# Norms of the attention stage on POOL, statistics spread over steps, and first units in the node units' order

## The chip, the cores and the metric

The kernel runs on one core of a Trainium2 chip. The metric is the device time of one execution in microseconds (us). The engines are PE (TensorE: matmuls, transposes), DVE (VectorE), ACT (ScalarE), POOL (GpSimd) and SP (SyncE, which here only issues DMAs). They run their own instruction streams in order and meet at semaphores.

## The reference

Input x is (8, 512, 128) in fp32. Four layers follow each other, each `x = layernorm(x + layer(x))`:

```
x = ln(x + mamba_like(x))          # conv, gating, a scan over the batch axis
x = ln(x + mixture_of_8_experts(x))
x = ln(x + attention(x))           # 16 heads of 8, softmax over 512 tokens, no output projection
x = ln(x + dag_of_6_nodes(x))      # below
```

The last layer makes six nodes. Each takes three earlier nodes, passes them through an edge matrix and a bias, does an attention of 8 heads of 16, multiplies with Wo and adds the scaled result to q:

```
q = ew[c,0]*(nodes[in_q] @ We[eq] + be[eq]);  k, v likewise
nodes[c] = act_w[c] * (softmax(qh kh^T / 4) vh @ Wo[c]) + q
```

Node 5 is then normalised, multiplied by ln_g, ln_b is added, then the layer's input, and the sum is normalised again: that is the output.

## The kernel before, in words

The first two layers take up some 380 us. The change touches what comes after, the attention stage, which is a row of 64 units. A unit is one batch element and eight heads. Units 0 to 15 are *first units* (third layer: 8 batch elements times two halves of the heads), units 16 to 63 are *node units* (six nodes times 8). The last eight, 56 to 63, are *final units*: their output is normed. `at_(c, q, r)` gives unit 4q + r; `x.half` is 1 for the odd first units, which complete a batch element; `x.b` is the batch element; `final(x)` gives 0 to 7 for a final unit and None for another.

Each engine runs a `body(c, q, r)` for every unit, with an order written out by hand: two halves k (four heads each) of eight steps i. A step is written (k, i) below. In each step PE does two score matmuls (`scores`, L1035, into the two banks of bank_s), whose rows DVE reduces to a negated maximum (`reduce`, L1394), and two matmuls of transposed scores (`scoresT`, L1058, into one of the two slots of bank_x), from which ACT makes the exponentials (`exp`, L825). The score matmuls and reductions run 36 tiles ahead of the transposed ones (`LEAD`). A score matmul waits until the reduction two tiles back is done. `slot()` hands out the two slots of bank_x in turn; whoever takes one waits for the reader of the last content. `misc()` does the same for bank_m.

Further work hangs on certain steps:

- `output` (L1075), probabilities times values, into bank_o. In node units it is two calls per four heads and two key tiles with 512 columns each (steps 0, 1 and 4, 5), in first units four calls with 256 columns (steps 0 to 7). The third argument of `paced(x, node, first)` is the step in a first unit, the second the step in a node unit.
- `turn` (L1089) transposes the result after ACT's copy `ev_pv` (L793); DVE's `divide` (L1505, L1512) writes it, divided by the sums, to ctx_sb.
- `value`, `proj_q`, `proj_kh`, `proj_qh` (L1021, L987, L1000, L1008) project for later units; each takes a slot of bank_x, and ACT copies it out (L775, L746, L756 or L759, L767).
- Node units: `turn_ctx` (L1099) at (0,6) transposes ctx_sb into a slot of bank_x, ACT copies it (`ev_cT`, L801), `out_proj` (L1109) at (0,7) multiplies with Wo into bank_m, and DVE's `node_out` (L1525) at (1,0) adds q. `maxima` (L1045) at step 1 transposes the maxima into bank_m, ahead of the step's outputs; SP writes them from there (`rows_m`) for the transposed scores of the next half.
- Odd first units, done during the even unit that follows: DVE adds the residual (`residual` step 0, L1535) at (0,7), takes the statistics (L1274 four times, L1278 four times) at (1,0) and normalises (L1283 four times) at (1,3). In between POOL makes 1/std (`rstd`, L600 and L602). `turn_x3` (L1118) transposes the result at (1,7).
- Final units: DVE's `final_norm` takes statistics at (1,3) and normalises at (1,5) of the next unit, and does both again at (0,1) and (0,7) of the unit after; in between POOL does `rstd`, adds ln_b to x3 (L665), multiplies with ln_g (L667) and sums (L669) in `final_sum`. `turn_final` (L1129) at (1,1) is PE's part.
- POOL's `split` (L609, L611) makes two parts of k and q of the unit three ahead; SP stacks them (`stack`).

POOL's order in a unit is: rstd of the residual, final_sum, split, rstd of the last norm. SP's is: loads, store_out, rows_m, stack, store_x3.

The functions that the change touches:

Of the kernel before, what the change touches and what calls it, by code (L numbers as in the profile page):

```python
# [11 lines left out]
P = 128  # L12
# [39 lines left out]
def build(nc, a):  # L52
# [7 lines left out]
    with ExitStack() as ctx:  # L60
# [74 lines left out]
        ctx_sb = cut2(L)  # L135
        ctxT = cut2(L)
# [81 lines left out]
        def names(prefix, *ns):  # L218
            for n in ns:
# [16 lines left out]
              "x2in", "x3", "x3out", "mv", "rs", "ones")  # L236
# [75 lines left out]

        def paced(x, node, first):

            return node if x.c.node else first
# [44 lines left out]
        def _(sp):  # L360
# [190 lines left out]
            def body(c, q, r):  # L551
# [6 lines left out]
                store_out(at_(c, q, r - 2))  # L558
# [6 lines left out]
                store_x3(at_(c, q, r - 1))  # L565
            units(sp, body)
# [11 lines left out]
        def _(pool):  # L578
# [50 lines left out]
            def residual_rstd(x):  # L629
# [28 lines left out]
            def final_sum(x):  # L658
# [12 lines left out]
            def final_rstd(x):  # L671

                j = final(x)
                if j is None:
                    return
                rstd(mv2, rs20, rs2, eps_ln[:, :], (S["f_mv2"], j + 1), (S["f_rs2_link"], j + 1), S["f_rs2"])

            def body(c, q, r):
# [5 lines left out]
            end = at_(kn, QU - 1, RING - 1)  # L684
            final_sum(end)
            final_rstd(end)
# [5 lines left out]
        def _(act):  # L692
# [102 lines left out]
            def ev_cT(x):  # L795
# [5 lines left out]
                act.activation(ctxT, ring.take()[0][:, 0:L], ACT.Copy).then_inc(S["c_cT_ev"], 1)  # L801
# [103 lines left out]
        def _(pe):  # L905
# [156 lines left out]
            def output(x, k, kp, step, steps):  # L1062


                if x is None or not 0 <= step < steps:
                    return
                G = 2 * x.u + k
                j, cols = 2 * step // steps, slice(0, L) if steps == 2 else slice(step % 2 * L // 2, (step % 2 + 1) * L // 2)
                if step == 0:
# [4 lines left out]
                for h in range(GH):  # L1074
                    mm = pe.matmul(bank_o[COL * h:COL * (h + 1), cols], vaug[x.half][:, 2 * kp + j, GH * k + h, :],  # L1075
                                   PT[:, kp, h, j, cols], start=(kp == 0 and step == 0),
                                   stop=(kp == 1 and step == steps - 1))
                if step == steps - 1:
# [13 lines left out]
            def turn_ctx(x):  # L1092
# [4 lines left out]
                to = slot(S["c_cT_ev"], x.un + 1)  # L1097
                for t in range(NT):
                    mm = pe.transpose(to[:, t * P:(t + 1) * P], ctx_sb[:, t * P:(t + 1) * P], ident[:, :])  # L1099
# [118 lines left out]
            def body(c, q, r):  # L1218
                x, last, ahead = at_(c, q, r), at_(c, q, r - 1), at_(c, q, r + 3)
                steps = paced(x, 2, 4)  # L1220
                for k in range(2):
                    for i in range(8):
# [3 lines left out]
                        scores(*two)  # L1226
                        if i == 1:
                            maxima(*led_group(c, q, r, k))
                        output(*((last, 1) if k == 0 else (x, 0)), 1, i, steps)
                        output(x, k, 0, i - 4, steps)  # L1230
                        if i == paced(x, 3, 5):
                            turn(*((last, 1) if k == 0 else (x, 0)))
                        if k == 0:
                            if i == paced(x, 2, 7):
# [18 lines left out]
            for step in range(2):  # L1253
                output(end, 1, 1, step, 2)
# [9 lines left out]
        def _(dve):  # L1264
# [232 lines left out]
            def divide(x, k, step):  # L1497
# [12 lines left out]
                dst = ctx_sb.rearrange("p (t m) -> p t m", t=NT)[:, :, first:first + w]  # L1510
# [16 lines left out]
            def residual(x, step):  # L1527

                x = only(x, False)
                if x is None or not x.half:  # L1530
                    return
                if step == 0:
                    need(dve, S["c_x2in"], 16 * x.b + 16)
                    need(dve, S["c_ot_ev"], 4 * x.b + 4)
                    dve.tensor_tensor(ctx_sb, ctx_sb, x2s, ALU.add).then_inc(S["c_xlink"], 1)  # L1535
                if step == 1:
                    need(dve, S["c_xlink"], (NT + 1) * x.b + 1)
                    stats(ctx_sb, stt, mv, S["c_xlink"], (NT + 1) * x.b + 1, S["c_mv"])
                if step == 2:
                    need(dve, S["c_rs"], x.b + 1)  # L1540
                    need(dve, S["c_x3T_ps"], x.b)
                    need(dve, S["c_x3out"], 16 * x.b)
                    normalise(x3s, ctx_sb, mv, rs, S["c_x3"])

            def final_norm(x, step):

                j = final(x)
                if j is None:
                    return
                if step == 0:  # L1550
                    need(dve, S["f_tT_ev"], j + 1)
                    stats(nT, stt, mv, S["f_link"], NT * j, S["f_mv"])
                if step == 1:
                    need(dve, S["f_rs"], j + 1)
                    need(dve, S["f_y"], j)
# [106 lines left out]
```

## Time and profile before

| | |
|---|---|
| median of 3 runs | 2267.18 us (2262.42 to 2274.65) |
| profiled execution | 2264.24 us, span 2262.2 us |
| PE busy | 2081.8 us, 92% of the span |
| DVE busy | 1745.5 us, 77% |
| ACT busy | 1478.8 us, 65% |
| POOL busy | 341.8 us, 15% |
| mean granted clock of PE | 0.944 |

The span is the time from the first instruction to the last on the profiled core. Busy time is the union of an engine's instructions; matmuls are pipelined and their ends are modelled, so a busy PE isn't PE at its peak. A line such as L1283 is the line of the kernel that issued the instruction, which for norms is that of a helper. The granted clock is a share of 2.4 GHz; in the records it is either 1.0 or 0.5.

### The profile page before, as it was taken

Reading aid. Unit: us, or ns where it says so; the run is one execution under the profiler, and the core shown is the slowest. Engines: PE = TensorE matmul, PEld = TensorE weight load, DVE = VectorE, ACT = ScalarE, POOL = GpSimd, SP = SyncE. Lnnn points to the kernel's source line nnn. Section 1 sums busy time; section 2 is a strip of 40 time slices with the busy share of each in tenths; the row PEclk is TensorE's granted clock in tenths of the full one; section 3 lists DMA queues with packets and bytes.
Section 4 is the critical chain, followed back from the end, with each engine's and each line's share of the span. In section 5 each row is a group of like instructions: output and inputs, shape, how many; then the busy total and the mean of one; then the engine's idle time right before and its main releaser. Section 6 shows DMA issues by size and latency. Waiting matters only on the chain.

```text
span 2262.2 us, 34032 instructions
## 1 busy us (share of the span) xinstructions
PE 2081.8 (92%) x11820; PEld 868.5 (38%) x11820; DVE 1745.5 (77%) x3501; ACT 1478.8 (65%) x2004; POOL 341.8 (15%) x385
## 2 busy tenths in 40 slices
PE   6747886999999999999999999999999999999995
PEld 2224442444344443333443334333333343333332
DVE  5846887677778777777777777777777777778884
ACT  4733552566666667777777777777777777776664
POOL 1102222000000011111111111111111111113223
PEclk9977786799899999999999999999999999999998
DMA  3001114133233345565655556555665565655630
GB/s 101 19 23 60 49 50 72 44 72 71 53 66 70 77 96 109 115 107 107 107 108 105 109 107 107 107 108 107 108 107 107 105 109 106 109 107 98 97 57 24
DMA packets 137206, 195.76 MB, mean 87 GB/s; under 512 B 20153, under 2 KB 55633, under 8 KB 137041
## 3 DMA queue, kind: packets, MB, share of 16 engines
q1 hardware_dynamic: 137040, 193.63, 43.9%
q8 instruction: 95, 1.56, 0.3%
q14 instruction: 71, 0.57, 0.1%
HBM read 75.45 MB, written 23.73 MB: 44 GB/s over the span
## 4 chain that ended last, share of the span: by engine, by line
PE 74%; DVE 16%; issue 5%; ACT 3%; POOL 1%; DMA 0%; DVEq 0%; POOLq 0%; SPq 0%; ACTq 0%
PE bank_s L1035 24%; PE bank_o L1075 20%; DVE nm L1394 6%; PE bank_x L1058 6%; PE bank_m L1089 3%; PE bank_x L1021 3%; PE bank_x L1000 3%; PE bank_x L1008 2%; ACT big L825 2%; PE bank_x L987 2%; DVE big L1283 2%; PE bank_m L1109 2%; PE bank_x L1135 2%; DVE big L1525 1%; PE bank_s L938 1%
## 5 line engine op out<-in xcount | busy, mean ns | idle before, releaser
L1394 DVE TENSOR_REDUCE nm<-bank_s 128x1 f32<-128x512 f32 x2048 | 1337.0, 684 | 361.7 <-PE bank_s L1035 355.6
L825 ACT ACTIVATE big<-bank_x 128x1024 f32<-128x1024 f32 x1024 | 1047.1, 1023 | 462.8 <-PE bank_x L1058 447.4
L1035 PE MATMUL bank_s<-kst,qst 48*128 48x512 f32 x2048 | 848.7, 473 | 39.9 <-DVE nm L1394 36.2
L1058 PE MATMUL bank_x<-qst,kst 50*128 50x512 f32 x2048 | 755.6, 450 | 5.3 <-ACT big L825 1.9
L1035 PEld LDWEIGHTS bank_s<-kst,qst 48*128 48x128 f32 x2048 | 356.5, 188 | 711.6 <-DVE nm L1394 640.0
L1075 PE MATMUL bank_o<-big,at 128*32 128x512 f32 (+1 forms) x5104 | 582.4, 529 | 3.2 <-ACT big L825 2.0
L1058 PEld LDWEIGHTS bank_x<-qst,kst 50*128 50x128 f32 x2048 | 306.2, 188 | 29.0 <-ACT big L825 22.5
L609 POOL CAST at<-at 128x512 fp32r<-128x512 f32 x112 | 68.2, 609 | 1295.2 <-ACT at L756 1028.9
L1075 PEld LDWEIGHTS bank_o<-big,at 128*32 128x32 f32 x5104 | 102.3, 109 | 175.3 <-issue 155.7
L611 POOL TENSOR_TENSOR at<-at 128x512 fp32r<-128x512 f32 x112 | 143.3, 1279 | 10.0
L793 ACT ACTIVATE at<-bank_o 128x512 f32<-128x512 f32 x128 | 76.4, 597 | 37.5 <-PE bank_o L1075 37.5
L1089 PE MATMUL bank_m<-ident,at 128*128 128x128 f32 x512 | 85.8, 291 | 1.0 <-ACT at L793 0.7
L833 ACT ACTIVATE big<-bank_x,big 128x128 f32<-128x128 f32 x256 | 68.9, 377 | 27.2 <-issue 11.6
L600 POOL TENSOR_TENSOR big<-big,eps_ln 128x4 f32<-128x4 f32 x40 | 13.7, 341 | 459.2 <-DVE big L1278 459.2
L1283 DVE TENSOR_SCALAR big<-big 128x128 f32<-128x128 f32 x192 | 68.1, 469 | 15.7 <-POOL big L602 14.8
L1135 PE MATMUL bank_x<-xw,big 128*128 128x512 f32 x128 | 79.5, 768 | 0.0
L1089 PEld LDWEIGHTS bank_m<-ident,at 128*128 128x128 f32 x512 | 54.8, 143 | 50.2 <-issue 47.9
L1478 DVE TENSOR_REDUCE big<-big 128x128 f32<-128x1024 f32 x32 | 61.1, 1908 | 10.2 <-ACT big L833 9.9
L1008 PE MATMUL bank_x<-at 128*128 128x512 f32 x96 | 52.8, 632 | 3.5
L1109 PE MATMUL bank_m<-big,at 128*128 128x512 f32 x96 | 55.0, 655 | 0.7 <-issue 0.7
L1021 PE MATMUL bank_x<-at 128*128 128x128 f32 x384 | 55.6, 288 | 0.0
L987 PE MATMUL bank_x<-at 128*128 128x512 f32 x96 | 53.9, 643 | 0.8 <-ACT big L817 0.8
(151 smaller groups left out, 1501.8 us busy)
## 6 DMA issues: line engine op xcount, KB each, us to landing
at<-nodes_d SPq DMA_DIRECT2D x144, 256.0 KB, 5.2
kst<-at SPq DMA_DIRECT2D x288, 128.0 KB
qst<-at SPq DMA_DIRECT2D x288, 128.0 KB
nodes_d<-big SPq DMA_DIRECT2D x48, 256.0 KB, 3.0
at<-w_d SPq DMA_DIRECT2D x48, 193.0 KB, 5.2
at<-x2T_d SPq DMA_DIRECT2D x32, 256.0 KB, 4.3
kst<-at SPq DMA_DIRECT2D x128, 64.0 KB
qst<-at SPq DMA_DIRECT2D x128, 64.0 KB
```

The lines of the kernel that those rows point to most:

```text
L611: pool.tensor_tensor(dst[:, 1, :], src, dst[:, 0, :], ALU.subtract).then_inc(done, n)
L825: act.activation(PT[:, kp, h, :, :], ring.take()[0].rearrange("p (c n) -> p c n", c=2), ACT.Exp, scale=x.c.scale).then_inc(S["c_ex"], 1)
L987: pe.matmul(to[:, 0:L], t[:, 0:P], t[:, WA:WA + L], start=True, stop=True).then_inc(S["c_qT_ps"], 1)
L1021: mm = pe.matmul(to[:, k * n:(k + 1) * n], t[:, P + k * P:P + (k + 1) * P], w, start=True, stop=True)
L1035: pe.matmul(bank_s[:, n % 2, :], qst[rows, x.r, h, t * P:(t + 1) * P], kst[rows, x.r, h, :], start=True, stop=True).then_inc(S["c_s_ps"], 1)
L1058: mm = pe.matmul(sec(to, j), kst[rows, x.r, h, kc_ * P:(kc_ + 1) * P], qst[rows, x.r, h, :], start=True, stop=True)
L1075: mm = pe.matmul(bank_o[COL * h:COL * (h + 1), cols], vaug[x.half][:, 2 * kp + j, GH * k + h, :], PT[:, kp, h, j, cols], start=(kp == 0 an ...
L1089: mm = pe.transpose(bank_m[:, t * P:(t + 1) * P], ot_sb[:, t * P:(t + 1) * P], ident[:, :])
L1109: pe.matmul(bank_m[:, :], st_o[x.half][:, 0:P], ctxT, start=True, stop=True).then_inc(S["c_wo_ps"], 1)
L1135: mm = pe.matmul(sec(bank_x[:, t % 2, :], j), hT[:, t * P:(t + 1) * P], xw[:, j * 512:(j + 1) * 512], start=True, stop=True)
L1283: i = dve.tensor_scalar(dst[:, t * D:(t + 1) * D], src[:, t * D:(t + 1) * D], mv_[:, t, 0:1], rs_[:, t:t + 1], ALU.subtract, ALU.mult)
L1394: dve.tensor_reduce(nm[:, k, at_n:at_n + 1], bank_s[:, n % 2, :], AX.X, ALU.max, negate=True).then_inc(S["c_red"], 1)
```

## The change

- DVE's residual sum goes to POOL (`residual_sum`). For it ctx_sb gets a second buffer (`ctx_two`), by the batch element's parity.
- All normalisations of the attention stage go to POOL (`normalise` there, four tensor_scalar of 128x128 each).
- DVE's statistics are no longer one piece of eight instructions but six pieces of one bn_stats or two bn_aggr (`tile_stats`), put in the steps listed below.
- `paced` and the split of `output` into four calls go: first units have the order of node units. In all units `output` now stands before `maxima`.
- `turn_ctx` writes bank_m in place of a slot of bank_x.
- POOL's order is now residual_sum, residual_norm, final_out of the unit two back, split, final_sum; in final_sum the sum with ln_b comes first. SP's store_out stands at the end of the unit.

```diff
+        ctx_two = (ctx_sb, sb("ctx_odd", [P, L])[:, :])
 # SP
-                store_out(at_(c, q, r - 2))
                 ahead, nxt = at_(c, q, r + 3), at_(c, q, r + 1)
...
                 store_x3(at_(c, q, r - 1))
+                store_out(at_(c, q, r - 2))
 # POOL
+            def normalise(dst, src, mv_, rs_, done):
+                for t in range(NT):
+                    i = pool.tensor_scalar(dst[:, t * D:(t + 1) * D], src[:, t * D:(t + 1) * D], mv_[:, t, 0:1], rs_[:, t:t + 1],
+                                           ALU.subtract, ALU.mult)
+                i.then_inc(done, 1)
+            def residual_sum(x):
...
+                to = ctx_two[x.b % 2]
+                need(pool, S["c_x2in"], 16 * x.b + 16)
+                need(pool, S["c_ot_ev"], 4 * x.b + 4)
+                pool.tensor_tensor(to, to, x2s, ALU.add).then_inc(S["c_xsum"], 1)
+            def residual_norm(x):
...
                 rstd(mv, rs0, rs, eps_ln[:, :], (S["c_mv"], x.b + 1), (S["c_plink"], x.b + 1), S["c_rs"])
+                need(pool, S["c_rs"], x.b + 1)
+                need(pool, S["c_x3T_ps"], x.b)
+                need(pool, S["c_x3out"], 16 * x.b)
+                normalise(x3s, ctx_two[x.b % 2], mv, rs, S["c_x3"])
...
-                rstd(mv, rs0, rs, eps_node[:, :], (S["f_mv"], j + 1), (S["f_rs_link"], j + 1), S["f_rs"])
                 need(pool, S["f_x3_in"], 16 * (j + 1))
                 pool.tensor_tensor(x33, x33, b3, ALU.add).then_inc(S["f_plink"], 1)
+                rstd(mv, rs0, rs, eps_node[:, :], (S["f_mv"], j + 1), (S["f_rs_link"], j + 1), S["f_rs"])
+                need(pool, S["f_rs"], j + 1)
+                normalise(zn, nT, mv, rs, S["f_nm"])
...
             def body(c, q, r):
-                residual_rstd(at_(c, q, r - 1))
+                residual_sum(at_(c, q, r - 1))
+                residual_norm(at_(c, q, r - 1))
+                final_out(at_(c, q, r - 2))
+                split(at_(c, q, r + 3))
                 final_sum(at_(c, q, r - 1))
-                split(at_(c, q, r + 3))
-                final_rstd(at_(c, q, r - 1))
 # ACT
-                act.activation(ctxT, ring.take()[0][:, 0:L], ACT.Copy).then_inc(S["c_cT_ev"], 1)
+                act.activation(ctxT, bank_m[:, :], ACT.Copy).then_inc(S["c_cT_ev"], 1)
...
-                        if i == paced(x, 1, 3):
+                        if i == 1:
                             ev_pv(*((last, 1) if k == 0 else (x, 0)))
 # PE
-                to = slot(S["c_cT_ev"], x.un + 1)
+                misc(S["c_cT_ev"], x.un + 1)
...
+                        output(*((last, 1) if k == 0 else (x, 0)), 1, i)
+                        output(x, k, 0, i - 4)
                         if i == 1:
                             maxima(*led_group(c, q, r, k))
-                        output(*((last, 1) if k == 0 else (x, 0)), 1, i, steps)
-                        output(x, k, 0, i - 4, steps)
-                        if i == paced(x, 3, 5):
+                        if i == 3:
                             turn(*((last, 1) if k == 0 else (x, 0)))
                         if k == 0:
-                            if i == paced(x, 2, 7):
+                            if i == 2:
                                 value(at_(c, q, r + 1))
 # DVE
+            def tile_stats(src, st_, mv_, ready, link, base, done, step):
+                if step < NT:
+                    need(dve, *ready)
+                    dve.bn_stats(st_[:, step, :], src[:, step * D:(step + 1) * D]).then_inc(link, 1)
+                    return
+                need(dve, link, base + NT)
+                for t in (2 * (step - NT), 2 * (step - NT) + 1):
+                    i = dve.bn_aggr(mv_[:, t, :], st_[:, t, :])
+                if step == NT + 1:
+                    i.then_inc(done, 1)
...
-                            if i == paced(x, 4, 6):
+                            if i == 4:
                                 divide(*((last, 1) if k == 0 else (x, 0)), j)
...
+                        for step, place in enumerate(((0, 6), (0, 7), (1, 0), (1, 1), (1, 2), (1, 3))):
+                            if (k, i) == place:
+                                residual_stats(last, step)
+                        for step, place in enumerate(((1, 3), (1, 4), (1, 5), (1, 6), (1, 6), (1, 7))):
+                            if (k, i) == place:
+                                node_stats(last, step)
+                        for step, place in enumerate(((0, 4), (0, 5), (0, 6), (0, 7), (0, 7), (1, 0))):
+                            if (k, i) == place:
+                                sum_stats(older, step)
```

## Rows read from the trace of the kernel before

**Rows 1.** The chain that ended last, by engine (page, part 4).
```profile
PE 74%; DVE 16%; issue 5%; ACT 3%; POOL 1%; DMA 0%; DVEq 0%; POOLq 0%; SPq 0%; ACTq 0%
```
**Rows 2.** Windows: length, busy PE, PEld, DVE, ACT, POOL, clock, DMA, GB/s; units 7, 8, 30, 58.
```profile
610.40:637.30 26.90, 26.55 (x216) 11.33 (x220) 21.66 (x41) 18.61 (x23) 1.89 (x2) 1.00 0.33 85
637.30:668.60 31.30, 29.11 (x220) 12.49 (x224) 25.23 (x54) 19.22 (x24) 3.09 (x4) 0.95 0.31 58
1239.60:1267.70 28.10, 27.71 (x162) 11.14 (x165) 22.27 (x42) 20.73 (x25) 3.70 (x5) 1.00 0.50 108
2057.40:2089.00 31.60, 30.03 (x163) 11.78 (x162) 27.68 (x66) 21.30 (x27) 9.90 (x12) 1.00 0.58 104
```
**Rows 3.** Single lines: durations min/median/max in ns, first and last start; L1525 from 930.4 to 2026.7.
```profile
L1535 DVE TENSOR_TENSOR big<-big x8: 678/680/681, 469.7 to 882.5; 128x512 f32<-128x512 f32 x8
...
L1525 DVE SCALAR_TENSOR_TENSOR big<-bank_m,at x39: 739/742/743, 945.2 to 2013.4; 128x512 f32<-128x512 f32 x39
```
**Rows 4.** Timeline (start, length, idle before and its releaser): unit 8, then unit 62.
```profile
657.06 1.29 DVE L1394 TENSOR_REDUCE nm<-bank_s 128x1 f32<-128x512 f32 x2 [1.36 <-PE bank_s L1035]
658.27 2.01 DVE L1283 TENSOR_SCALAR big<-big 128x128 f32<-128x128 f32 x4
...
660.94 0.49 PE L1035 MATMUL bank_s<-kst,qst 48*128 48x512 f32 x1 [1.38 <-DVE nm L1394]
...
2206.26 0.86 DVE L1274 BATCH_NORM_STATS2 big<-big 128x6 f32<-128x128 f32 x4
...
2207.28 0.38 DVE L1278 BATCH_NORM_AGGREGATE big<-big 128x2 f32<-128x6 f32 x4 [0.16 <-DVE big L1274]
...
2211.69 1.26 DVE L1493 TENSOR_TENSOR mp<-nm,mp 128x16 fp32r<-128x16 f32 x1
```
**Rows 5.** Waits of PE, 930.4 to 2026.7: us in total, times, longest.
```profile
PE bank_m L1045 <- DVE big L1525: 9.1, 39, 0.2
```
**Rows 6.** Timeline of unit 38, from turn_ctx to step (1,0).
```profile
1502.81 0.66 PE L1099 MATMUL bank_x<-ident,big 128*128 128x128 f32 x4
1502.92 1.02 ACT L825 ACTIVATE big<-bank_x 128x1024 f32<-128x1024 f32 x1 [0.65 <-PE bank_x L1058]
...
1503.84 0.59 ACT L801 ACTIVATE big<-bank_x 128x512 f32<-128x512 f32 x1
...
1504.66 1.13 PE L1109 MATMUL bank_m<-big,at 128*128 128x512 f32 x2
1504.76 1.02 ACT L825 ACTIVATE big<-bank_x 128x1024 f32<-128x1024 f32 x1 [0.33 <-PE bank_x L1058]
1506.48 1.02 ACT L825 ACTIVATE big<-bank_x 128x1024 f32<-128x1024 f32 x1 [0.70 <-PE bank_x L1058]
```
**Rows 7.** Timeline of ACT, end of unit 38, steps (1,6), (1,7), (0,0), (0,1).
```profile
1517.02 1.02 ACT L825 ACTIVATE big<-bank_x 128x1024 f32<-128x1024 f32 x1 [0.67 <-PE bank_x L1058]
...
1518.86 1.02 ACT L825 ACTIVATE big<-bank_x 128x1024 f32<-128x1024 f32 x1
1520.05 0.60 ACT L767 ACTIVATE at<-bank_x 128x512 f32<-128x512 f32 x1 [0.16 <-PE bank_x L1008]
1520.77 1.02 ACT L825 ACTIVATE big<-bank_x 128x1024 f32<-128x1024 f32 x1
1522.43 1.02 ACT L825 ACTIVATE big<-bank_x 128x1024 f32<-128x1024 f32 x1 [0.64 <-PE bank_x L1058]
```
**Rows 8.** POOL's lines in the whole trace: busy us, mean ns of one, idle before.
```profile
L609 POOL CAST at<-at 128x512 fp32r<-128x512 f32 x112 | 68.2, 609 | 1295.2 <-ACT at L756 1028.9 <-ACT at L759 214.7 <-issue 41.8
L602 POOL TENSOR_TENSOR big<-big,half 128x4 f32<-128x4 f32 x48 | 48.5, 1010 | 3.8
L669 POOL TENSOR_TENSOR big<-big 128x512 f32<-128x512 f32 x8 | 10.1, 1267 | 0.6
```
**Rows 9.** Timeline of DVE, the last normalisation.
```profile
2258.31 1.11 DVE L1283 TENSOR_SCALAR big<-big 128x128 f32<-128x128 f32 x4 [1.41 <-POOL big L602]
```
**Rows 10.** Window of unit 0, columns as in rows 2.
```profile
396.90:430.90 34.00, 33.12 (x181) 13.91 (x182) 21.06 (x39) 18.14 (x21) 1.89 (x2) 0.61 0.10 31
```

More of the change, by code:

```diff
@@ L627, in split @@
                     in_parts(qf, qp, base + 1, S["c_sp"], 1)
-            def residual_rstd(x):
+            def normalise(dst, src, mv_, rs_, done):
[4 more added lines that the diff above has]
+            def residual_sum(x):
+                x = only(x, False)
+                if x is None or not x.half:
+                    return
[4 more added lines that the diff above has]
+            def residual_norm(x):
                 x = only(x, False)
@@ L1060, in scoresT, with output @@
                 mm.then_inc(S["c_st_ps"], 1)
-            def output(x, k, kp, step, steps):
-                if x is None or not 0 <= step < steps:
+            def output(x, k, kp, j):
+                if x is None or not 0 <= j < 2:
                     return
                 G = 2 * x.u + k
-                j, cols = 2 * step // steps, slice(0, L) if steps == 2 else slice(step % 2 * L // 2, (step % 2 + 1) * L // 2)
-                if step == 0:
+                if j == 0:
                     need(pe, S["c_ex"], 8 * G + 4 * kp + 4)
@@ L1074, in output @@
                 for h in range(GH):
[L1075 to L1078, printed above, removed]
+                    mm = pe.matmul(bank_o[COL * h:COL * (h + 1), :], vaug[x.half][:, 2 * kp + j, GH * k + h, :],
+                                   PT[:, kp, h, j, :], start=(kp == 0 and j == 0), stop=(kp == 1 and j == 1))
+                if j == 1:
                     mm.then_inc(S["c_pv_ps"], 1)
@@ L1253, in _ @@
             for step in range(2):
-                output(end, 1, 1, step, 2)
+                output(end, 1, 1, step)
             turn(end, 1)
@@ L1509, in divide @@
                 first = k * w if x.c.node else x.half * 2 * w + k * w
-                dst = ctx_sb.rearrange("p (t m) -> p t m", t=NT)[:, :, first:first + w]
+                to = ctx_sb if x.c.node else ctx_two[x.b % 2]
+                dst = to.rearrange("p (t m) -> p t m", t=NT)[:, :, first:first + w]
                 need(dve, S["c_sum"], G + 1)
@@ L1525, in node_out @@
                 dve.scalar_tensor_tensor(no_sb, bank_m[:, :], st_o[x.half][:, P:P + 1], q_sb[x.r], ALU.add, ALU.add).then_inc(S["c_wo_ev"], 1)
-            def residual(x, step):
-                x = only(x, False)
[L1530 to L1543, printed above, removed]
@@ L1545, in final_norm @@
[L1545 to L1563 removed]
+            def tile_stats(src, st_, mv_, ready, link, base, done, step):
+                if step < NT:
+                    need(dve, *ready)
+                    dve.bn_stats(st_[:, step, :], src[:, step * D:(step + 1) * D]).then_inc(link, 1)
+                    return
+                need(dve, link, base + NT)
[3 more added lines that the diff above has]
+                    i.then_inc(done, 1)
@@ new lines, in residual_stats, with node_stats, sum_stats @@
+            def residual_stats(x, step):
+                x = only(x, False)
+                if x is not None and x.half:
+                    tile_stats(ctx_two[x.b % 2], stt, mv, (S["c_xsum"], x.b + 1), S["c_xlink"], NT * x.b, S["c_mv"], step)
+            def node_stats(x, step):
+                j = final(x)
+                if j is not None:
+                    tile_stats(nT, stt, mv, (S["f_tT_ev"], j + 1), S["f_link"], NT * j, S["f_mv"], step)
+            def sum_stats(x, step):
+                j = final(x)
+                if j is not None:
+                    tile_stats(zn, stt2, mv2, (S["f_z"], j + 1), S["f_link2"], NT * j, S["f_mv2"], step)
@@ L1576, in body @@
             def body(c, q, r):
-                x, last = at_(c, q, r), at_(c, q, r - 1)
+                x, last, older = at_(c, q, r), at_(c, q, r - 1), at_(c, q, r - 2)
                 for k in range(2):
```

49 lines of the change are left out of this document (16 added, 33 removed).

## The prediction

> **What bounds the kernel now.** I read the chain of waits first: 74% of it is PE, 16% DVE [rows 1]. Then I cut the trace into units at every sixteenth exponential of L825 and looked at four of them as windows [rows 2]. The reader is to see three kinds of unit. An ordinary node unit takes 28.1 us with PE busy 27.7 of it; the repeat of L1525 gives the same, (2013.4 - 945.2) / 38 = 28.11 us [rows 3]. A first unit without residual takes 26.9 us, again all PE (26.55). But a first unit that carries a residual takes 31.3 us while PE has work for 29.1 at a clock of 0.95, and a final node unit takes 31.6 with PE busy 30.0 and DVE 27.7 against 22.3. From L1535 a pair of first units takes (882.5 - 469.7) / 7 = 58.97 us [rows 3]. So PE sets the pace, and where DVE does a norm in one piece PE stands still behind it.
>
> How one piece of DVE work stops PE: four L1283 take 2.01 us in the middle of the reductions, and the next score matmul starts after 1.38 us of idle time whose releaser is L1394 [rows 4]. Only two score banks exist, so a piece longer than the slack of one step (two reductions are 1.29 us, [rows 4]; a step with outputs is 1.66, 1520.77 to 1522.43, [rows 7]) goes straight into PE's time. Short pieces in steps with outputs cost nothing.
>
> **Part 1, maxima behind the outputs (all node units).** At step 1 of the second half PE waits for the DVE of node_out: 9.1 us in 39 units, 0.23 each [rows 5]. Putting the output matmuls in between hides it whole: a step with outputs is 1.66 us against 1.29 for two reductions [rows 4, 7], so they take longer than 0.23. 47 units (16 to 62): -0.23 x 47 = -10.8 us. Bounds: 0, if the later mT copy holds the next exponential on ACT, to -12. What is late next is PE itself.
>
> **Part 2, turn_ctx into bank_m (node units).** Every take of an extra slot of bank_x makes the next scoresT wait for the exponential just before it. This is why steps with a slot last 1.84 us whatever PE does in them: 1502.92 to 1504.76 with turn_ctx, 1517.02 to 1518.86 with proj_kh, 1518.86 to 1520.77 with proj_qh [rows 6, 7]. The change takes the slot away, but out_proj still needs ctxT, whose copy ends at 1503.84 + 0.59 = 1504.43, and out_proj now starts at 1504.66 [rows 6]. With a hand-over of 0.08 that is -0.15, not the 0.5 that the missing slot suggests. -0.15 x 47 = -7 us. Bounds: 0 to -0.23 x 47 = -11.
>
> **Part 3, first units in the node order.** Now every step holds half an output, and the unit is even. In the node order eight of sixteen steps hold a whole output and eight none. The steps with none stay at the 1.29 of two reductions, the slots for value and proj_kh and the transposes move into such steps. I take the node unit, 28.1, subtract part 1 (0.25), and replace the four steps that first units don't fill: turn_ctx 1.84, out_proj 1.72 (1504.76 to 1506.48), proj_kh 1.84 and proj_qh 1.91 [rows 6, 7], by two of 1.3 and two of 1.5 that also hold parts: 28.1 - 0.25 - 7.31 + 5.6 = 26.1. For the clock, which can fall in the thinner steps, I add 0.3: 26.4 against 26.9 now. Bounds: 25.6 to 28.5 (all eight thin steps at 1.66).
>
> A residual unit adds to that: turn_x3 makes a step of 1.3 to 1.84 (+0.55); four bn_stats of 0.86 / 4 = 0.22 and two pairs of bn_aggr of 0.38 / 2 [rows 4], of which two stats and one pair stand in thin steps, with one link wait of 0.16 (+0.8); the port and the clock +0.55. That is 28.3. Gone are L1535 (0.68, [rows 3]), the stats in one piece (0.86 + 0.16 + 0.38 = 1.4) and L1283 (2.01). A pair is then 26.4 + 28.3 = 54.7 against 58.97, so -4.3 x 7 = -30 us for units 2 to 16; the rest of units 0, 1 and 16 I leave at 0. Bounds of the pair: 52.5 to 59.
>
> **Part 4, the norms of the final units.** A final unit is 28.1 + 0.66 for the four transposes of turn_final (as L1099, [rows 6]) + DVE pieces: each of the two sets of statistics puts one or two stats beside parts or divide (about 0.5 us over the slack), +1.1 together: 29.9 against 31.6, so -1.7 in each of five units and -1.5 for the two at the ends: -10 us. Two sets of L1283 leave DVE (1.11 us alone, [rows 9], 2.01 beside POOL, [rows 4], each), which is where it comes from. Bounds: -16 to +3.
>
> What POOL pays: residual sum 1.27 (L669, [rows 8]) beside two steps of slack before the first bn_stats. One normalise of 128x128 on POOL the trace doesn't show. Bounds: a quarter of the cast L609, 0.15, and the whole two-input L669, 1.27; nearest is a one-input op of a quarter of L609's size plus a start, I take 0.35, four are 1.4 us. Then residual_norm is rstd (0.2 + 1.01, L602) + 1.4 = 2.7 us after step (1,3) and turn_x3 at (1,7) comes some 6 us later: hidden; at 1.27 each it is 6.3 and just late. split(r+3) waits behind it by about 3 us; its scores start more than a unit later, so nobody waits, and the same holds for SP, whose store_out now stands behind the stack.
>
> The tight place is final_sum. It now stands behind both splits. qf is copied at 1520.05 + 0.60, just before the unit ends [rows 7]; cast and subtract (0.61 + 1.27), bias sum 1.27, rstd 1.3, normalise 1.4, product and sum 2 x 1.27: f_z comes 8 us into the next unit, and DVE asks for it at step (0,4), after 6.6 + 1.3 + 0.4 = 8.3 us. It fits by a hair; if normalise takes 0.6 instead of 0.35, it is 1 us late in six units, 6 us.
>
> **Part 5, the tail.** DVE's four L1283 take 1.11 us alone [rows 9] and 2.01 beside a POOL op [rows 4]; of the two sets in the tail the first stands beside POOL's bias sum, which now comes earlier. POOL does each in 1.4: -0.6 and +0.3. The order of last's statistics is off the path. Sum 0, bounds -2 to +4.
>
> **Sum.** -10.8 - 7 - 30 - 10 + 0 = -58 us. The profiled execution took 2264.24 us (span 2262.2 and 2.0 around it), 2.9 under the median 2267.18: 2206 in its own terms, 2209 against the median.
>
> **A rule of the skill against it.** Row: with POOL in a 1.26 us op, L1493, a subtraction of 16 columns, took 1.26 us at 2211.69 [rows 4]. The Trainium skill, "SBUF — State Buffer", section "SBUF: two separate sides", says that GpSimd and a VectorE op with two SBUF inputs or in a two-port mode hold a shared port pair exclusively, for the whole instruction. The trace agrees. It speaks against giving POOL the norms, and is the rival B below.
>
> **The rivals.** A: the node order is wrong for first units. Now their PE work is even; after, a full step of 1.66 alternates with a thin one in which PE waits for DVE. For it: the residual unit with the 1.38 us of idle time had a mean granted clock of 0.95, part of it at 1.2 GHz [rows 2, 4]. Against it: node units, whose steps alternate too, hold 1.00 [rows 2]. If it costs 1.5 us in each of 16 units, the sum is -58 + 24 = -34: 2233 us. The Trainium skill, "TensorE: Matmul & The Clock Gate", section "A second HAM failure mode: psum-queue depth-cycling", describes just such micro-idles between groups as making the clock oscillate; the trace shows a lower clock only in units with whole stalls.
>
> B: POOL becomes the bound. Its split, moved to the steps (1,5) and (1,6) of residual units, runs into parts (up to +1.1 x 7 = 8), and f_z is late by 1 to 2 us in six units (+9); part 4's gain is then gone: 2209 + 17 = 2226. For it: L1493's 1.26 us. Against: POOL is busy 3.1 and 9.9 us of a unit now [rows 2].
>
> C, slower: the clock stays low through the first units. Unit 0 at a mean clock of 0.61 took 34.0 us [rows 10] against 27.3 as I forecast the mean: 6.7 per unit. Nine such units eat the 58 us; all sixteen give 2209 + 107 = 2316, ten to twelve 2276 to 2289. Against: with a stall of 1.38 us the unit's mean clock was still 0.95, and the forecast stalls are shorter.
>
> D: both A and B in full, with parts 1 and 2 at nothing: -58 + 24 + 17 + 17 = 0, about 2267.
>
> **Chances.** Forecast 0.68 (own range 2195 to 2222), A 0.13, B 0.10, D 0.04, C 0.05. Under 0.5% (11 us) a measurement of this kernel can't tell a change from none. Faster 0.91, same 0.04, slower 0.05. Range 2184 to 2238, which takes in A and B and the lower bounds of parts 3 and 4 together.
>
> **What would show it.** Right: node units at 27.7 us; steps with turn_ctx no longer 1.84; no idle time of L1045 behind L1525; residual units at 28.3 and other first units at 26.4, with the clock at 1.00 nearly throughout; final units at 29.5; POOL's TENSOR_SCALAR at 0.35 us. Wrong: first units over 27.5 with the clock falling in steps 6 and 7; DVE idle in front of L1274 at (0,4), released by L669; POOL's op over 0.6 us.

## The result

The changed kernel takes 2252.99 us (median of 10 runs, 2242.97 to 2260.7), the kernel before 2263.14 us in the same comparison (10 runs). The ratio is 0.9943, 95% interval 0.9915 to 0.9972: by the ratio about 13 us faster (6 to 19), by the medians 10, where 58 were forecast. The profiled executions differ by 13 us, spans 2262.2 and 2249.2 us.

The same four cuts through both traces, at the starts of units 1, 16, 57 and 63, say where the 13 us are. Windows of the changed kernel: units 1 to 15, units 16 to 56, units 57 to 62, unit 63 with the tail (columns as in [rows 2]):

```profile
430.70:874.10 443.40, 423.09 (x2266) 165.43 (x2268) 329.17 (x657) 291.25 (x343) 71.01 (x83) 0.89 0.35 74
874.10:2010.40 1136.30, 1131.90 (x6480) 461.32 (x6484) 911.33 (x1689) 853.84 (x1026) 158.37 (x172) 1.00 0.60 109
2010.40:2196.30 185.90, 173.81 (x954) 69.04 (x949) 142.56 (x330) 124.35 (x151) 81.86 (x98) 0.94 0.46 81
2196.30:2249.20 52.90, 28.61 (x143) 9.98 (x143) 9.75 (x48) 20.01 (x25) 34.76 (x42) 0.75 0.11 30
```

The same units in the kernel before, with their clock:

```profile
430.90:873.00 442.10, 426.65 (x3225) 180.56 (x3228) 348.12 (x692) 287.27 (x344) 40.49 (x48) 0.96 0.35 75
873.00:2026.70 1153.70, 1136.61 (x6480) 457.75 (x6477) 915.70 (x1694) 849.73 (x1025) 153.80 (x166) 1.00 0.58 107
2026.70:2213.40 186.70, 173.82 (x954) 68.81 (x954) 160.90 (x374) 123.62 (x150) 51.74 (x59) 0.98 0.49 82
2213.40:2262.20 48.80, 27.20 (x143) 9.83 (x143) 17.05 (x68) 20.04 (x25) 14.50 (x17) 0.80 0.10 28
```

| stretch | forecast | measured | clock before, after |
|---|---|---|---|
| units 1 to 15 | -30 | +1.3 | 0.96, 0.89 |
| units 16 to 56 | -15.6 | -17.4 | 1.00, 1.00 |
| units 57 to 62 | -12 | -0.8 | 0.98, 0.94 |
| unit 63 and tail | 0 | +4.1 | 0.80, 0.75 |

The forecast of -12 is part 4 (-10) and six units of parts 1 and 2. The remaining 0.2 us lie ahead of unit 1. Of the 45 us that are missing from the forecast, 31 are in the first units, 11 in the final units and 4 in the tail. Parts 1 and 2 came as forecast; 1.0 of the 17.4 us is unit 16 alone, which still carries a residual (29.3 us before, 28.3 after). In the first units DVE is free of its long pieces and lost 19 us of busy time, and yet nothing is gained: the clock is the column that got worse.

Two first units and two windows of 3.4 us of the changed kernel show how. The third window is the end of a residual unit (thin steps, then turn_x3), the fourth the start of the next unit, at half the clock:

```profile
550.80:578.70 27.90, 26.43 (x149) 10.49 (x148) 21.42 (x41) 18.84 (x22) 1.89 (x2) 0.93 0.40 101
639.00:670.50 31.50, 30.02 (x157) 11.66 (x160) 22.88 (x49) 19.48 (x24) 7.47 (x9) 0.83 0.22 40
666.70:670.10 3.40, 2.85 (x16) 1.66 (x14) 3.07 (x7) 2.65 (x3) 3.19 (x4) 1.00 0.00 0
670.10:673.50 3.40, 3.40 (x19) 0.74 (x18) 1.50 (x3) 1.02 (x1) 0.00 (x0) 0.50 0.19 58
```

And ACT's exponentials in the same place:

```profile
667.18 1.02 ACT L851 ACTIVATE big<-bank_x 128x1024 f32<-128x1024 f32 x1 [0.63 <-PE bank_x L1084]
668.47 1.03 ACT L851 ACTIVATE big<-bank_x 128x1024 f32<-128x1024 f32 x1 [0.26 <-PE bank_x L1084]
...
670.47 1.02 ACT L851 ACTIVATE big<-bank_x 128x1024 f32<-128x1024 f32 x1 [0.38 <-PE bank_x L1084]
673.57 1.02 ACT L851 ACTIVATE big<-bank_x 128x1024 f32<-128x1024 f32 x1 [2.08 <-PE bank_x L1084]
```

L851 is what L825 was. The reader is to see the step of 3.10 us (670.47 to 673.57). It holds one whole output, as the steps of 1.66 us do, and it runs at 1.2 GHz: its eight output matmuls (L1099) take 1.93 us together, where the next eight, at full clock again, take 1.07. The clock fell just behind the thin steps. The steps themselves are those of the forecast. In units without residual, where the clock is 1.00, their medians in the first half are 1.72, 1.87, 1.84, 1.25, 1.91, 1.66, 1.28 and 1.42 us, 12.9 together. The second half differs mainly in its first step, 1.96, and takes 13.2. The sum is 26.2 us, and 26.1 were forecast.

In the final units POOL is what is new. Timeline, from the start of unit 59 at 2072.3:

```profile
2075.58 0.21 POOL L597 TENSOR_TENSOR big<-big,eps_node 128x4 f32<-128x4 f32 x1
2075.87 1.03 POOL L599 TENSOR_TENSOR big<-big,half 128x4 f32<-128x4 f32 x1
2077.01 3.13 POOL L629 TENSOR_SCALAR big<-big 128x128 f32<-128x128 f32 x4
2080.22 1.29 POOL L688 TENSOR_TENSOR big<-big,lngb 128x512 f32<-128x512 f32 x1
...
2082.88 0.29 DVE L1554 BATCH_NORM_STATS2 big<-big 128x6 f32<-128x128 f32 x1 [2.54 <-POOL big L690]
```

Four tensor_scalar on POOL (L629) take 3.13 us. The sum L690 is ready 10.5 us into the unit; DVE has waited for it since 8.0, and its reductions stand behind that wait. PE runs out of work too, and the clock falls behind that stall as well (0.50 from 2086.6 to 2090.0).

### The profile page after: what moved, and what is told of

It reads as the page before. It is cut to its first block, busy times and chain, and to the rows that moved or that the text cites. A ratio compares the mean times of both kernels' runs of the same rounds, so it can differ in the third digit from the quotient of the medians.

```text
span 2249.2 us, 31985 instructions
## 1 busy us (share of the span) xinstructions
PE 2069.6 (92%) x10812; PEld 854.9 (38%) x10812; DVE 1696.8 (75%) x3397; ACT 1487.1 (66%) x2004; POOL 427.3 (19%) x489
## 4 chain that ended last, share of the span: by engine, by line
PE 81%; DVE 9%; issue 4%; POOL 4%; ACT 1%; DMA 1%; DVEq 0%; POOLq 0%; SPq 0%; ACTq 0%
PE bank_s L1061 27%; PE bank_o L1099 23%; PE bank_x L1084 7%; PE bank_m L1112 3%; PE bank_x L1047 3%; PE bank_x L1026 3%; PE bank_m L1132 2%; DVE nm L1416 2%; PE bank_x L1034 2%; PE bank_x L1013 2%; PE bank_s L964 1%; PE bank_x L1158 1%; PE bank_m L1122 1%; PE bank_m L1071 1%; POOL big L629 1%
## 5 line engine op out<-in xcount | busy, mean ns | idle before, releaser
L851 ACT ACTIVATE big<-bank_x 128x1024 f32<-128x1024 f32 x1024 | 1047.9, 1024 | 503.5 <-PE bank_x L1084 477.0
L1084 PE MATMUL bank_x<-qst,kst 50*128 50x512 f32 x2048 | 764.1, 454 | 1.6 <-ACT big L851 1.6
L1061 PEld LDWEIGHTS bank_s<-kst,qst 48*128 48x128 f32 x2048 | 365.1, 191 | 689.4 <-DVE nm L1416 581.2
L1099 PE MATMUL bank_o<-big,at 128*32 128x512 f32 x4096 | 578.4, 639 | 2.2 <-ACT big L851 2.0
L606 POOL CAST at<-at 128x512 fp32r<-128x512 f32 x112 | 68.2, 609 | 1243.4 <-ACT at L782 1030.5
L608 POOL TENSOR_TENSOR at<-at 128x512 fp32r<-128x512 f32 x112 | 143.3, 1279 | 10.1 <-POOL at L606 0.5
L1099 PEld LDWEIGHTS bank_o<-big,at 128*32 128x32 f32 x4096 | 82.6, 110 | 161.0 <-issue 157.1
L859 ACT ACTIVATE big<-bank_x,big 128x128 f32<-128x128 f32 x256 | 68.7, 376 | 29.5 <-issue 15.3
L1158 PE MATMUL bank_x<-xw,big 128*128 128x512 f32 x128 | 74.8, 727 | 1.6 <-ACT big L859 1.6
L629 POOL TENSOR_SCALAR big<-big 128x128 f32<-128x128 f32 x80 | 62.5, 794 | 2.1
L1071 PEld LDWEIGHTS bank_m<-ident,mp 128*32 128x32 f32 x128 | 12.1, 95 | 118.3 <-issue 116.6
L1034 PE MATMUL bank_x<-at 128*128 128x512 f32 x96 | 52.6, 630 | 4.0
```

Of the source, the lines that this page charges most:

```text
L608: pool.tensor_tensor(dst[:, 1, :], src, dst[:, 0, :], ALU.subtract).then_inc(done, n)
L629: i = pool.tensor_scalar(dst[:, t * D:(t + 1) * D], src[:, t * D:(t + 1) * D], mv_[:, t, 0:1], rs_[:, t:t + 1], ALU.subtract, ALU.mult)
L851: act.activation(PT[:, kp, h, :, :], ring.take()[0].rearrange("p (c n) -> p c n", c=2), ACT.Exp, scale=x.c.scale).then_inc(S["c_ex"], 1)
L1034: pe.matmul(to[:, 0:L], st_qk[x.half][:, P:2 * P], q_sb[x.r], start=True, stop=True).then_inc(S["c_qh_ps"], 1)
L1061: pe.matmul(bank_s[:, n % 2, :], qst[rows, x.r, h, t * P:(t + 1) * P], kst[rows, x.r, h, :], start=True, stop=True).then_inc(S["c_s_ps"], 1)
L1084: mm = pe.matmul(sec(to, j), kst[rows, x.r, h, kc_ * P:(kc_ + 1) * P], qst[rows, x.r, h, :], start=True, stop=True)
```

## The experiments

**Even order.** The changed kernel with `paced` and the four output calls back for first units:

```diff
-                        output(*((last, 1) if k == 0 else (x, 0)), 1, i)
-                        output(x, k, 0, i - 4)
+                        output(*((last, 1) if k == 0 else (x, 0)), 1, i, steps)
+                        output(x, k, 0, i - 4, steps)
...
-                        if i == 3:
+                        if i == paced(x, 3, 5):
                             turn(*((last, 1) if k == 0 else (x, 0)))
```

> The changed kernel, but first units have their old order again (four output calls of 256 columns per key pair, divide at step 6, turn at 5, value at 7); residual and norms stay on POOL, the six pieces of statistics at (0,7), (1,0), (1,1), (1,2) twice and (1,3). Theory 'clock': first units lost their gain because PE does too little in the steps without an output and its clock falls; with the even order the clock stays at 1.00, a first unit without residual takes 26.9 us, one with residual 28.5, a pair 55.4 instead of 58.9, units 2 to 16 together 25 us less: about 2228. Rival 'pieces': the loss is from POOL's and DVE's pieces of the residual, whatever the order; the pair stays at 58 to 59 and the time at 2250.

Measured: 2223.57 us, ratio 0.9767 (0.9683 to 0.9852), where the theory said 2228. Windows of a unit without residual, one with, and units 1 to 15:

```profile
542.60:569.50 26.90, 26.56 (x216) 11.30 (x218) 21.65 (x41) 18.81 (x22) 1.89 (x2) 1.00 0.42 104
569.50:597.20 27.70, 27.18 (x221) 11.81 (x224) 23.68 (x49) 19.43 (x24) 7.47 (x9) 1.00 0.26 45
433.40:846.40 413.00, 407.26 (x3225) 174.36 (x3228) 339.00 (x657) 290.25 (x343) 71.15 (x83) 1.00 0.37 80
```

A pair is 54.6 us, against 58.97 in the kernel before [rows 3]. Units 1 to 15 take 413.0 us, 29 less than before and 30 less than in the changed kernel, at a clock of 1.00. So moving the residual to POOL and cutting the statistics up is worth the 4.3 us per pair of the forecast, and the new order took it away. Part of the 4.3 is the clock, which was 0.96 over these units in the kernel before. What POOL and what the cut statistics give by themselves no run separates.

**Filler.** The changed kernel with work added in the thin steps:

```diff
+                        busy = k == 1 and not x.c.node and (ahead.c.node or (i == 7 and last is not None and last.half))
+                        if i >= 6 and not x.c.node and not busy:
+                            if reader[0] is not None:
+                                need(pe, *reader[0])
+                            pe.matmul(bank_m[:, 0:256], xw[:, 0:P], xw[:, 0:256], start=True, stop=True)
```

> The changed kernel with one added fp32 matmul of 256 columns, whose result nobody reads, into the free bank_m in steps 6 and 7 of each half of a first unit (where no other extra stands). Theory 'clock': it fills the thin steps, which DVE sets, at no cost of its own; the clock stays at 1.00 in the first units, which then take 26.1 us and 27.6 with residual; a pair 53.7 instead of 58.9, together 36 us less: about 2217. Rival 'pieces': the added matmul is only more work, up to 0.4 us in each of 60 steps, nothing gained: 2250 to 2275.

Measured: 2207.33 us, ratio 0.9687 (0.9611 to 0.9763). Windows: a unit without residual, one with, units 1 to 15, and the whole stretch in which the clock did not fall once:

```profile
534.20:560.70 26.50, 26.50 (x160) 11.20 (x164) 21.14 (x41) 18.88 (x23) 1.89 (x2) 1.00 0.42 106
560.70:587.40 26.70, 26.70 (x159) 11.47 (x152) 22.68 (x49) 19.41 (x23) 7.49 (x9) 1.00 0.19 47
427.70:829.80 402.10, 401.82 (x2360) 170.15 (x2364) 328.85 (x657) 291.44 (x344) 71.07 (x83) 1.00 0.37 82
410.70:2008.10 1597.40, 1590.61 (x9164) 655.22 (x9161) 1286.13 (x2438) 1187.32 (x1418) 245.09 (x271) 1.00 0.54 101
```

With matmuls whose result nobody reads, units 1 to 15 take 402.1 us in the trace and not 443.4, 41 us less. The medians differ by 46 us, but they are from two comparisons, and the kernel before was 13 us slower in this one than in the one of the result. A pair is 53.3 us, better than with the even order. This settles the rival 'pieces': POOL's and DVE's pieces of the residual are the same in this kernel.

**Order alone.** The kernel before, with its first units in the node units' order and nothing else:

```diff
-            return node if x.c.node else first
+            return node
```

> The kernel before with the order of its first units changed to that of node units and nothing else (residual still on DVE in three pieces). Theory 'clock': units without residual take 28 to 29 us as in the changed kernel, with the clock falling at steps 0 and 8, instead of 26.9; with residual 31 to 33; together 10 to 20 us more than before: about 2275 to 2285. Rival 'pieces': units without residual take the 26.1 us of the steps' sum and the kernel is 5 us faster than before.

Measured: 2273.57 us against 2276.38 in that comparison, ratio 0.9965 (0.9926 to 1.0005). The 10 to 20 us more that were expected lie outside this interval. The profiled execution, 2280.47 us, is the slowest of its ten (2257.31 to 2280.47). Its windows, the last of them units 1 to 15:

```profile
679.60:707.00 27.40, 25.94 (x148) 10.27 (x148) 21.25 (x41) 18.65 (x23) 1.89 (x2) 0.95 0.33 82
707.00:741.00 34.00, 31.58 (x157) 12.03 (x160) 25.22 (x54) 19.34 (x23) 3.09 (x4) 0.79 0.31 53
428.90:888.80 459.90, 433.61 (x2266) 167.74 (x2268) 345.77 (x692) 288.90 (x344) 40.35 (x48) 0.87 0.34 72
```

A pair is 61.4 us against 58.97, and the clock of the residual unit 0.79 against 0.95 [rows 2]. The unit without residual came out at 27.4, under the 28 expected. Units 1 to 15 take 459.9 us here and 442.1 in the trace of the kernel before. But this trace is of the longest of ten executions, that of the kernel before (2264.24 us) is near the shortest of its own, and the times show no loss. So it is shown that the clock falls in first units of this order with the residual still on DVE, and not shown that the order alone costs time.

**Later statistics.** The changed kernel with

```diff
-                        for step, place in enumerate(((0, 4), (0, 5), (0, 6), (0, 7), (0, 7), (1, 0))):
+                        for step, place in enumerate(((0, 6), (0, 7), (1, 0), (1, 1), (1, 2), (1, 3))):
```

> The changed kernel with the second set of statistics of final units two steps later, at (0,6), (0,7), (1,0), (1,1), (1,2), (1,3), so that DVE no longer asks for the sum before POOL has it. Theory 'late sum': the 2.5 us of DVE idle in front of the first bn_stats goes, and with it the fall of the clock behind it; final units 57 to 61 take 29.3 us instead of 31.8 to 33.5, some 12 us less in all: about 2240. Rival 'port': DVE is slowed by sharing its port with a POOL that is busy half the unit; then the units stay above 31 us.

Measured: 2246.66 us, ratio 0.984 (0.9768 to 0.9911). The first window is final unit 59, the second unit 63 up to its last matmuls:

```profile
2067.20:2095.80 28.60, 28.40 (x166) 11.43 (x170) 24.21 (x58) 21.28 (x27) 16.21 (x20) 1.00 0.56 115
2181.70:2222.00 40.30, 38.16 (x125) 12.12 (x129) 4.55 (x21) 18.56 (x22) 19.37 (x24) 0.51 0.07 20
```

Final units take 28.6 us, less than the 29.5 of the prediction, with POOL as busy as before (16.2 us): the rival 'port' is out. Units 57 to 62 together are 14.5 us shorter than in the changed kernel. But in this trace as much was given back in unit 63: the clock fell 0.5 us after its start and stayed at 1.2 GHz for 41 us, so it took 67.2 us with the tail and not 52.9. The expected 2240 had left this out.

Unit 63 holds no score matmuls. That alone does not make the clock fall. In the trace of the kernel before it holds the same kinds of matmul, and the clock stayed at 1.00 from its start to the tail:

```profile
2213.40:2242.70 29.30, 24.04 (x137) 8.61 (x137) 10.63 (x43) 19.34 (x24) 8.32 (x10) 1.00 0.10 28
```

**Two norms of four.** The changed kernel with `for t in range(0, NT, 1 if first else 2)` in POOL's `normalise`:

> The changed kernel with two of the four tensor_scalar of each norm on POOL left out from the second batch element on (half of each norm is not computed), so that a norm costs 1.6 us there, about what was forecast for four. If the late sum is the price of that op, it comes 1.6 us earlier: the step (0,5) of final units takes 2.1 instead of 3.66 us, the clock doesn't fall behind it, and units 58 to 61 take 29 us instead of 32 to 33.5. Rival: the place behind both splits makes it late whatever the norm costs; then (0,5) stays over 3 us.

Measured: 2246.8 us, one run. The step (0,5) takes 2.13 us and unit 59

```profile
2072.00:2100.90 28.90, 28.31 (x166) 11.42 (x164) 24.21 (x58) 21.36 (x26) 13.03 (x16) 1.00 0.58 114
```

28.9 instead of 32.1, clock 1.00. So at about the price that was forecast for a norm, 1.4 us, the place behind the splits would have cost the step half a microsecond (2.13 for 1.66); at 3.13 it cost 2 us plus the clock.

**Forms of POOL's op.** Each of the four column groups gets another form:

```diff
+                    if t == 1:
+                        i = pool.tensor_scalar(to, of, 0.5, 2.0, ALU.subtract, ALU.mult)
+                    if t == 2:
+                        i = pool.tensor_scalar(to, of, mv_[:, t, 0:1], None, ALU.subtract)
+                    if t == 3:
+                        i = pool.tensor_tensor(to, of, mv_[:, t, 0:1].broadcast_to([P, D]), ALU.subtract)
```

> The changed kernel with four forms of the op in each norm on POOL (the values are not those of a norm): both scalars from memory; both immediate; one from memory and one operation; and a tensor_tensor against a column repeated 128 times. Theory 'scalars': the 0.79 us are for two operations with scalars from memory, the immediate form takes 0.3 and the form with one about 0.5. Rival 'start': POOL needs some 0.6 us for any op of this class, and all forms take 0.6 to 0.8, the tensor_tensor 0.45.

Measured (columns as in [rows 8]; L631 the old form, L633 immediates, L635 one operation, L637 tensor_tensor):

```profile
L631 POOL TENSOR_SCALAR big<-big 128x128 f32<-128x128 f32 x20 | 16.0, 798 | 2.1
L633 POOL TENSOR_SCALAR big<-big 128x128 f32<-128x128 f32 x20 | 12.8, 642 | 0.0
L635 POOL TENSOR_SCALAR big<-big 128x128 f32<-128x128 f32 x20 | 12.1, 605 | 0.0
L637 POOL TENSOR_TENSOR big<-big 128x128 f32<-128x128 f32 x20 | 8.0, 400 | 0.0
```

The numbers of the rival 'start' held: 0.60 us for the leanest tensor_scalar. Two operations take 0.64 with immediate scalars and 0.80 with scalars from memory, so most of the 0.2 goes with the scalars from memory. A two-input tensor_tensor of the same size is cheaper, 0.40. Whether the 0.6 us are a fixed start isn't shown, since tensor_scalar ran at one size only. For tensor_tensor a start of 0.6 us is out. L608, in the same trace, takes 1.28 us for four times the columns; a line through 0.40 and 1.28 leaves a start of 0.1 us (an estimate, as the two forms differ).

**Parts 1 and 2 alone,** in the kernel before: `output` moved ahead of `maxima`, and `to = bank_m` after `misc(...)` in turn_ctx with ACT reading bank_m.

> The kernel before with one edit: the outputs of step 1 stand before the maxima. If part 1 of the prediction is right, the wait of L1045's counterpart behind node_out goes and an ordinary node unit takes 27.87 us instead of 28.11 (the step (1,1) 1.9 instead of 2.18). Rival: the 0.40 us that node units gained are all from the missing slot; then 28.11 stays.

> The kernel before with one edit: turn_ctx goes through bank_m instead of a slot of bank_x. If part 2 is right, a node unit takes 27.95 us, steps (0,6) and (0,7) 3.4 together instead of 3.56. By the rival that the slot was the whole gain it takes 27.7.

Measured, one run each, 2257.56 and 2259.34 us; windows of one node unit (28.11 before):

```profile
1273.10:1300.90 27.80, 27.64 (x162) 11.27 (x166) 22.31 (x42) 20.92 (x25) 3.72 (x5) 1.00 0.63 108
```

```profile
1264.20:1292.20 28.00, 27.67 (x162) 11.18 (x162) 22.23 (x42) 20.59 (x26) 3.72 (x5) 1.00 0.62 107
```

The means of units 17 to 55 are 27.81 and 28.00 us. So -0.30 and -0.11 us, together the 0.41 of the changed kernel (27.70). The forecasts were -0.23 and -0.15.

**All together.** First the filler, the later statistics and, in unit 63, a matmul of 128 columns into bank_s in steps 2, 3, 6 and 7; second the same with the very last two norms back on DVE.

> The changed kernel with the filler of the earlier run in the first units, the second statistics of final units two steps later, and in the last unit, whose steps hold no score matmuls, one fp32 matmul of 128 columns into bank_s, which nobody reads any more, in steps 2, 3, 6 and 7. Theory 'clock': the filler run's 2207 less the 12 us of late sums, with unit 63 and tail at 51 and not the 67 of the run with later statistics: 2193. Rival: the clock falls before the last unit and stays low as it did there, and the gain of the later statistics is lost again: 2207.

> The same kernel with the two norms of the very last batch element back on DVE. POOL takes 3.18 us for four, DVE 1.11: 2 x 2.07 = 4.1 us of pure path in the tail, so 2189. Rival: bias sum and product on POOL slow DVE by the shared port as before and half of it is lost: 2191, not to be told from the kernel above in the times, only in the trace of the tail.

Measured: 2212.82 us, ratio 0.9751 (0.9711 to 0.979), and 2204.17, ratio 0.9715 (0.9674 to 0.9755). The first missed by 20 us. Unit 63 up to its last matmuls:

```profile
2139.60:2187.50 47.90, 46.98 (x145) 17.41 (x145) 4.55 (x21) 19.30 (x23) 19.47 (x24) 0.50 0.08 23
```

Its filler did not bring the clock back in 47.9 us with PE busy 47 of them; at 1.2 GHz PE is the bound and each added matmul costs its time. The tail's norms brought 8.7 us in the medians; 4.1 were expected, and the profiled unit 63 with its tail shows 73.0 against 68.7 us, a difference of 4.3. The other 4 us are not explained.

**Filler before the fall.** The same kernel, no filler in unit 63 but

```diff
+                        if (k, i) in ((1, 6), (1, 7)) and x.u in (U - 3, U - 2):
+                            need(pe, *reader[0])
+                            w = 256 if x.u == U - 3 else 128
+                            pe.matmul(bank_m[:, 0:w], xw[:, 0:P], xw[:, 0:w], start=True, stop=True)
```

> The last of the combined kernels (filler in the first units, later statistics, the very last norms on DVE) without the filler in unit 63; in its place one added fp32 matmul into bank_m in steps (1,6) and (1,7) of unit 61 (256 columns) and of unit 62 (128), where the score matmuls run out and just after which the clock fell. Theory 'before the fall': the clock must be kept up ahead of unit 63, since inside it more work only makes the slow clock dearer; then unit 63 runs at full clock, 47 us with the tail instead of 68.7, and the time is 2183. Rival 'fewer scores': without score matmuls unit 63 can't hold the clock whatever stands before it; then 62 to 64 us as with later statistics alone, 2198.

Measured: 2186.78 us, ratio 0.965 (0.9607 to 0.9692), all six runs within 2185.14 to 2188.23. Unit 63 starts at 2134.6 and takes 48.8 us with the tail. The window runs from inside unit 62 to the end of unit 63's steps:

```profile
2111.70:2159.50 47.80, 44.21 (x256) 17.74 (x258) 23.42 (x70) 34.77 (x40) 20.54 (x27) 1.00 0.11 31
```

This is the best kernel of the study, 75 us under the one before. The theory held (2183 expected) and the rival 'fewer scores' is out. The clock still fell once, at the start of unit 62, for 6.8 us, and came back; what did not happen is the fall at the start of unit 63. This kernel without any filler in units 61 to 63 was not run. The fall did come in all four profiled runs that had the later statistics without this filler.

**Even order with the other two repairs,** no filler anywhere.

> The changed kernel with the old, even order in the first units, the second statistics two steps later and the very last norms on DVE; no filler anywhere. From the even-order run (2223.6, units 58 to 61 of 33.5 us): 4 x 4 us less for the late sums, 4 us less in the tail, and if the clock falls before unit 63 as in the other runs with later statistics, up to 14 us more there: 2204 to 2218.

Measured: 2206.67 us (2198.25 to 2221.8), ratio 0.9741 (0.9686 to 0.9796). Within the range. In the profiled run the clock fell 1.1 us after the start of unit 63 and came back 24 us later; the unit took 58.2 us with the tail.

## Why the prediction was wrong

The range was 2184 to 2238 us and 2253 lies outside it; the sign was right. Part 3's term for the clock is the step that failed; parts 4 and 5 add a mis-sized op.

- *Part 1, maxima behind the outputs*: right, 0.30 for 0.23 us. *Part 2, the slot*: right in kind, 0.11 for 0.15; the missing stall is mostly given back at out_proj, as argued. Together 16.4 of the 17.4 us in units 16 to 56, where 15.6 were forecast.
- *Part 3, first units in the node order*: the step that failed. The steps' sum was right to 0.1 us (26.1). The wrong term is "for the clock, which can fall in the thinner steps, I add 0.3". It fell behind thin steps in nearly every first unit, once or twice, and a step with an output took 3.10 us at 1.2 GHz for 1.66. The mean clock of units 1 to 15 was 0.89, and they took 443.4 us where the forecast's 30 us less would have made it 412. Rival A named the mechanism and priced it at 1.5 us in 16 units, 24 us in all; the filler run puts it at 41 us in units 1 to 15. It had a chance of 0.13 and deserved more. The argument against it was that node units alternate too and hold 1.00. Their thin places hold projections, which first units lack; that this is why they hold their clock is likely by the filler run, but no run took work out of a node unit.
- *Part 3, residual on POOL*: right in size. With the even order the pair is 54.6 for the forecast 54.7, but this is partly luck: the forecast added up the steps of another order. It also took the kernel before at one mild unit. Its even units 2 to 14 took 31.1 to 33.8 us, and the clock fell in six of these seven.
- *Part 4*: the POOL op was sized 0.35 us, from a quarter of the cast L609 and a start, and took 0.79, more than the whole cast (0.61). The prediction had the tight place and the sign ("8 us into the next unit, and DVE asks for it after 8.3"): it asked at 8.0 and got it at 10.5. The price was put at 1 us per unit if the op took 0.6; the stall was 2.5 and the clock fell behind it, which a stall's price has to include. Without the stall the part is worth more than forecast, 28.6 for 29.5 us a unit.
- *Part 5, the tail*: the same op. Two norms of 3.13 us stand in place of DVE's 2.04 and 1.11, 3.1 us more, in a stretch that grew by 4.1 where 0 was forecast.
- *Rival B*: the lateness of f_z was B's, but it came from the price of the op and not from the port. The blocking of [rows 4] is there in the changed kernel too, only shorter. L1515, the line that was L1493, takes 0.17 us; in the six places where it ran beside a POOL op it took 0.40 and ended with that op (below). In the kernel before it took 0.83 us five times, beside L669, and 1.26 once. What also left is DVE's tensor_scalar, whose four took 2.01 us beside POOL and 1.11 alone.

```profile
487.79 0.61 POOL L606 CAST at<-at 128x512 fp32r<-128x512 f32 x1
488.03 0.40 DVE L1515 TENSOR_TENSOR mp<-nm,mp 128x16 fp32r<-128x16 f32 x1
```

- *Rival C* did not come: the clock never stayed low in the first units. It did in unit 63 of later kernels, a case that the prediction does not have. *Rival D* needed parts 1 and 2 at nothing, and both came.

What is open: why the clock recovers within 3 to 7 us in the first units and stays low for 24 to 48 us in unit 63 of the kernels with later statistics, with PE busy in both. The missing score matmuls are not enough as a reason. With the slot edit of part 2 alone the clock fell 1.7 us after the start of unit 63 and was back 3.4 us later:

```profile
2207.00:2210.40 3.40, 3.40 (x14) 0.81 (x13) 0.48 (x5) 1.77 (x3) 1.22 (x2) 0.50 0.00 0
2210.40:2230.80 20.40, 17.35 (x96) 6.43 (x98) 6.41 (x21) 15.44 (x17) 4.94 (x5) 1.00 0.09 27
```

The difference between single runs of one kernel goes with these falls for the most part: nine of the changed kernel's ten runs line up from 2243.0 us at a mean clock of 0.930 to 2260.7 at 0.921. The tenth, 2259.4 at 0.888, does not fit. What decides in which runs the clock falls is open too.

## What to carry to other kernels

Where another engine sets the pace of a step, PE's spare time in it isn't free: if a few such steps stand together, the clock can fall and the next full steps pay nearly double (3.10 us for 1.66 here). Spread the matmuls evenly, or fill the thin steps with some that nobody reads, ahead of the place where the clock would fall and not behind it. And size an op on a new engine by a run of that very op: the estimate from the nearest row in the trace was off by more than a factor of two, in the one place that had no slack. Dividing the cast's time by the size was the error; an op of a quarter of its size took as long as the whole cast.

## What the runs showed of the hardware that was not expected

- Useless fp32 matmuls, one of 256 columns in steps 6 and 7 of each half, kept PE at 2.4 GHz through the first units and made units 1 to 15 41 us shorter; the clock did not fall for 1597 us.
- On POOL a tensor_scalar of 128x128 takes 0.60 to 0.80 us by form, a tensor_tensor against a repeated column 0.40, though it has two inputs.
- In unit 63 the clock stayed at 1.2 GHz for 47.8 us while PE was busy nearly all the time; with small fillers in the last two steps of the two units before, it stayed at 2.4 GHz through the same unit's steps.
- A DVE op of 16 columns with two inputs from SBUF that met a POOL op ended when that op ended: 0.40 us beside the cast L606, 0.83 beside L669 and 1.26 beside L667, for 0.17 alone.
